# Where the transposed value products of an attention and FFN kernel are copied and normalised

## The reference

```python
q, k, v = split_heads(xn @ Wq + bq), split_heads(xn @ Wk + bk), split_heads(xn @ Wv + bv)   # 16 heads of 8
scores = einsum('bhqd,bhkd->bhqk', q, k) * 8 ** -0.5 + slopes[h] * rel[k]    # alibi, see below
ctx = einsum('bhqk,bhkd->bhqd', softmax(scores), v)
attention = ctx @ Wo + bo
# ffn: fp4_linear quantises both sides in blocks of 16 and multiplies
ffn = fp4_linear(silu(fp4_linear(xn, w_gate)) * fp4_linear(xn, w_up), w_down)
```

## Time and profile before

| What | us |
|---|---|
| median of 3 runs (lowest, highest) | 858.97 (858.61, 860.21) |
| profiled execution, its time | 858.46 |
| its span | 856.7 |
| PE busy | 778.5 (91%) |
| DVE busy | 695.4 (81%) |
| ACT busy | 652.2 (76%) |
| POOL busy | 416.5 (49%) |
| chain that ended last | PE 66%, DVE 17%, ACT 6%, POOL 6% |

### The profile page before, as it was taken

How to read it: one execution, slowest core, us unless ns; L and a number is a source line. 1 busy time by engine, 2 the same in 40 slices (tenths; PEclk the granted TensorE clock), 3 DMA queues, 4 the chain that set the end, 5 groups by cost and what they waited for, 6 DMA issues and landing times.

```text
span 856.7 us, 13894 instructions
## 1 busy us (share of the span) xinstructions
PE 778.5 (91%) x4939; PEld 232.0 (27%) x4939; DVE 695.4 (81%) x792; ACT 652.2 (76%) x1342; POOL 416.5 (49%) x413
## 2 busy tenths in 40 slices
PE   3289998989999999899899999999999999998986
PEld 2012232223232333222232333222222323232322
DVE  7797886888989897788888887888888898989710
ACT  4206886878888888778788888887888888888885
POOL 7365263482628373662545462761717362442442
PEclk9657998999999999989999999999999999999999
DMA  5920002013102010050101011050102000000000
GB/s 149 243 51 1 2 2 76 2 50 100 39 1 51 2 67 10 14 149 1 39 2 38 3 45 45 2 160 2 38 2 50 3 14 2 2 1 2 2 2 25
DMA packets 32828, 31.85 MB, mean 37 GB/s; under 512 B 4344, under 2 KB 26552, under 8 KB 32760
## 3 DMA queue, kind: packets, MB, share of 16 engines
q1 hardware_dynamic: 32760, 30.96, 13.4%
HBM read 15.91 MB, written 15.04 MB: 36 GB/s over the span
## 4 chain that ended last, share of the span: by engine, by line
PE 66%; DVE 17%; ACT 6%; POOL 6%; issue 3%; DMA 1%; SPq 0%; POOLq 0%; ACTq 0%; DVEq 0%
PE low L1078 23%; PE mx L1048 21%; DVE neg_max L934 13%; PE low L1067 6%; ACT probs L728 4%; PE low L1116 3%; PE low L1101 2%; PE low L1095 2%; PE low L1034 2%; PE mx L1127 2%; PE low L1108 2%; ACT pv_s L825 1%; POOL mb L537 1%; DVE am L905 1%; PE low L1030 1%
## 5 line engine op out<-in xcount | busy, mean ns | idle before, releaser
L934 DVE TENSOR_REDUCE neg_max<-mx 128x1 f32<-128x1024 f32 x512 | 614.1, 1220 | 99.5 <-PE mx L1048 91.4
L728 ACT ACTIVATE probs<-low 128x512 f32<-128x512 f32 x1024 | 558.7, 607 | 141.1 <-PE low L1067 135.2
L1048 PE MATMUL mx<-k_op,q_op 51*128 51x512 bf16 x1024 | 320.1, 398 | 42.0 <-DVE neg_max L934 21.8
L1067 PE MATMUL low<-q_op,k_op 53*128 53x512 bf16 x1024 | 334.4, 389 | 12.7 <-ACT probs L728 9.1
L1078 PE MATMUL low<-probs,v_op 128*32 128x512 f32 x2048 | 275.7, 611 | 0.3
L1048 PEld LDWEIGHTS mx<-k_op,q_op 51*128 51x128 bf16 x1024 | 61.8, 95 | 318.2 <-issue 171.5
L1067 PEld LDWEIGHTS low<-q_op,k_op 53*128 53x128 bf16 x1024 | 74.7, 93 | 91.6 <-ACT probs L728 81.9
L630 POOL CAST neg_parts<-neg_max 128x16 bf16<-128x16 f32 x31 | 6.8, 219 | 167.1 <-DVE neg_max L934 102.1
L537 POOL TENSOR_SCALAR mb<-mb 128x960 f32<-128x960 f32 (+2 forms) x17 | 58.7, 3456 | 27.5 <-DVE mb L925 26.2
L1078 PEld LDWEIGHTS low<-probs,v_op 128*32 128x32 f32 x2048 | 40.5, 108 | 67.5 <-issue 32.2
L618 POOL TENSOR_TENSOR x_s<-x_s,down_s 128x128 f32<-128x128 f32 x32 | 14.6, 455 | 80.5 <-ACT down_s L761 57.9
(11 more groups left out here) (128 smaller groups left out, 589.8 us busy)
## 6 DMA issues: line engine op xcount, KB each, us to landing
q_op<-q_rows SPq DMA_DIRECT2D x32, 192.0 KB, 3.8
k_op<-k_rows SPq DMA_DIRECT2D x32, 192.0 KB, 4.8
q_rows<-qp SPq DMA_DIRECT2D x8, 384.0 KB, 2.6
k_rows<-kp SPq DMA_DIRECT2D x8, 384.0 KB, 2.9
x_s<-in_L_attn_inputs_dram SPq DMA_DIRECT2D x8, 256.0 KB, 3.8
q_rows<-qp SPq DMA_DIRECT2D x8, 256.0 KB, 2.9
k_rows<-kp SPq DMA_DIRECT2D x8, 256.0 KB, 3.1
out_dram<-o_s SPq DMA_DIRECT2D x8, 256.0 KB, 2.6
```

The lines of the kernel that those rows point to most:

```text
L728: nc.scalar.activation(probs[U % 3][:, 2 * g + x, :], bank("exp", U, j), ACT.Exp).then_inc(st_free, 1)
L934: nc.vector.tensor_reduce(to, slot("max", pos)[:], AX.X, ALU.max, negate=True).then_inc(mx_free, 1)
L1048: ins = nc.tensor.matmul(slot("max", pos)[:, 512 * kh:512 * kh + 512], q, k, start=True, stop=True)
L1067: nc.tensor.matmul(bank("exp", U, j), k_op[quad][r, g, kt * P:(kt + 1) * P], q_op[quad][r, g, half * HALF:(half + 1) * HALF], start=True, ...
```

## The change

`pvT` leaves AT_END and IN_DVE_RING: it becomes a middle job whose transposes go to one of the three banks of the ring that ScalarE frees. ScalarE copies the bank back to `pv_s`, in SBUF (a new copy, 32 times, and the old content of `pv_s` has been read by then). VectorE's two operations become `context(m)`, run in the unit after the job's, behind the first maximum of that unit; they read `pv_s` and no longer PSUM, and signal a new semaphore `ctx_ok`. `ctxT` is asked for two units after the last pvT instead of one. The next copy of `pv` into `pv_s` waits for `ctx_ok`. Since the middle places are shared, the planner moves other jobs too.

```diff
--- before.py
+++ after.py
@@ -73,8 +73,8 @@
 CHUNKS = 2 * B * QUADS * UNITS
 HALVES = 2 * B * QUADS
 FFN_FIRST, FFN_LAST = 5, 237
-AT_END = ("turn", "pvT")
-IN_DVE_RING = ("pvT", "bvo")
+AT_END = ("turn",)
+IN_DVE_RING = ("bvo",)
 
 
 def turn_unit(m):
@@ -146,7 +146,7 @@
             assert U < parts_unit(g)
             put(max(U, QUADS * UNITS * (b - 1) + 2) + 1, "v", g)
     for hb in range(2 * B):
-        U = put(at["pvT", hb // 2 * 8 + 6 + hb % 2] + 1, "ctxT", hb)
+        U = put(at["pvT", hb // 2 * 8 + 6 + hb % 2] + 2, "ctxT", hb)
         for i in range(2):
             U = put(max(U, at["down", 2 * hb + 1, 1]) + 1, "wo", hb, i)
     return at
@@ -318,6 +318,7 @@
         hid_ok = sem("hid_ok")
         down_ok = sem("down_ok")
         out_ok = sem("out_ok")
+        ctx_ok = sem("ctx_ok")
         z_ok = sem("z_ok")
         pow_ok = sem("pow_ok")
         quant_ok = sem("quant_ok")
@@ -780,6 +781,9 @@
                     keep_v(p)
                 elif kind == "turn":
                     keep_turn(p)
+                elif kind == "pvT":
+                    full("pvT", p)
+                    nc.scalar.copy(pv_s[:], bank("pvT", p)).then_inc(st_free, 1)
                 elif kind == "ctxT":
                     full("ctxT", p)
                     if p:
@@ -821,7 +825,7 @@
                         m = U // KT - 1
                         act.wait_ge(pv_done, U - 1)
                         if m:
-                            act.wait_ge(mx_full, MX["pvT", m - 1] + 1)
+                            act.wait_ge(ctx_ok, m)
                         nc.scalar.copy(pv_s[:], pv).then_inc(pv_kept, 1)
                     for job in middle(U) if j == 1 else ():
                         job_on_scalar(job)
@@ -938,21 +942,22 @@
                     nc.vector.tensor_tensor(neg_parts[m % 2][:, 16:32], neg_max[m % 2][:], neg_parts[m % 2][:, 0:16],
                                             ALU.subtract).then_inc(parts_max_ok, 1)
 
+            def context(m):
+                b, quad, half = m // 8, m // 2 % QUADS, m % 2
+                dve.wait_ge(st_free, ST["pvT", m] + 1)
+                heads = pv_s[:].rearrange("p (t h c) -> p t h c", h=4, c=32)
+                if b >= 2 and quad == 0 and half == 0:
+                    dve.wait_ge(st_full, ST["ctxT", 2 * b - 3] + 1)
+                link(nc.vector.reciprocal(pv_r[:].rearrange("p (t h) -> p t h", h=4), heads[:, :, :, D]))
+                nc.vector.tensor_tensor(
+                    ctx_s[b % 2][:, 4 * half:4 * half + 4, 32 * quad:32 * quad + 32].rearrange(
+                        "p t (h d) -> p t h d", d=D), heads[:, :, :, 0:D],
+                    pv_r[:].rearrange("p (t h) -> p t h", h=4).unsqueeze(3).to_broadcast([P, 4, 4, D]),
+                    ALU.mult).then_inc(ctx_ok, 1)
+
             def job_on_vector(job):
                 kind, p = job[0], job[1] if len(job) > 1 else 0
-                if kind == "pvT":
-                    b, quad, half = p // 8, p // 2 % QUADS, p % 2
-                    full("pvT", p)
-                    heads = slot("pvT", p)[:, 0:512].rearrange("p (t h c) -> p t h c", h=4, c=32)
-                    if b >= 2 and quad == 0 and half == 0:
-                        dve.wait_ge(st_full, ST["ctxT", 2 * b - 3] + 1)
-                    link(nc.vector.reciprocal(pv_r[:].rearrange("p (t h) -> p t h", h=4), heads[:, :, :, D]))
-                    nc.vector.tensor_tensor(
-                        ctx_s[b % 2][:, 4 * half:4 * half + 4, 32 * quad:32 * quad + 32].rearrange(
-                            "p t (h d) -> p t h d", d=D), heads[:, :, :, 0:D],
-                        pv_r[:].rearrange("p (t h) -> p t h", h=4).unsqueeze(3).to_broadcast([P, 4, 4, D]),
-                        ALU.mult).then_inc(mx_free, 1)
-                elif kind == "bvo":
+                if kind == "bvo":
                     full("bvo")
                     link(nc.vector.tensor_tensor(bo_s[:], slot("bvo")[:, 0:P], bo_s[:], ALU.add))
                     dve.sem_inc(mx_free, 1)
@@ -986,6 +991,9 @@
                         job_on_vector(job)
                     if pos < CHUNKS:
                         reduce_chunk(pos)
+                    for job in JOBS.get(U - 1, ()) if i == 0 else ():
+                        if job[0] == "pvT":
+                            context(job[1])
                     for p in range(NP):
                         up0, up1 = AT["up", p, 0], AT["up", p, 1]
                         if (U, i) == (up0 + 1, 1):
@@ -1121,14 +1129,14 @@
                 elif kind == "turn":
                     turn(p)
                 elif kind == "pvT":
-                    free_slot("pvT", p)
+                    free_bank("pvT", p)
                     pe.wait_ge(pv_kept, p + 1)
                     for t in range(4):
-                        ins = nc.tensor.transpose(slot("pvT", p)[:, t * P:(t + 1) * P], pv_s[:, t * P:(t + 1) * P], ident[:])
-                    ins.then_inc(mx_full, 1)
+                        ins = nc.tensor.transpose(bank("pvT", p)[:, t * P:(t + 1) * P], pv_s[:, t * P:(t + 1) * P], ident[:])
+                    ins.then_inc(st_full, 1)
                 elif kind == "ctxT":
                     free_bank("ctxT", p)
-                    pe.wait_ge(mx_free, MX["pvT", p // 2 * 8 + 6 + p % 2] + 1)
+                    pe.wait_ge(ctx_ok, p // 2 * 8 + 6 + p % 2 + 1)
                     for t in range(4):
                         ins = nc.tensor.transpose(bank("ctxT", p)[:, t * P:(t + 1) * P],
                                                   ctx_s[p // 2 % 2][:, 4 * (p % 2) + t, :], ident[:])
```

## The result

| | before | changed |
|---|---|---|
| median of 5 runs each, us | 858.97 (856.29 to 860.21) | 862.96 (861.58 to 863.83) |
| ratio, 95% interval | | 1.0049 (1.0028 to 1.0069) |
| profiled execution, us / its span | 858.46 / 856.7 | 863.23 / 861.4 |

The account below looks back on a forecast made before the run. Neither DVE (81% busy) nor ScalarE (76%) fills the span, so the order of work matters. -3.5 - 6.0 - 4.8 + 12.9 + 4.6 + 0.6 = +3.8 us gave 862.8 us, range 855.5 to 868.

Parts of the forecast that it names:

- price list: Usual times between TensorE's value products, such as 2.46 us without a middle job and 2.95 with; 754.4 in all before.
- unit 40's pause: TensorE before hT of job 2: scale_back behind swish makes hT 3.6 us late, plus 2.0 for the clock: 5.6.
- unit 134's: TensorE before hT of job 8: scale_back behind swish makes hT 2.8 us late, plus 2.0 for the clock: 4.8.
- units 92 to 96: POOL's late hid there: up jobs move between its three_parts blocks, so 0.5 of 5.3 us stays, a gain of 4.8.
- pvT moves (-3.5): TensorE's units: 31 end jobs go (-18.0 us), 29 more middle jobs come (+14.2), plus 0.3; ScalarE's copies cost nothing extra.
- POOL's queue (+12.9): POOL's in-order work misses hT's new deadlines, with clock penalties behind the pauses: 5.6 + 4.8 + 1.7 + 0.8 us.
- The multiply waits for POOL (+4.6): DVE's multiply from SBUF waits out POOL's add in four contexts: 3.4 us, plus half of up to 2.4 for follow-up.
- DVE's share (-6.0): DVE's late small pieces shrink as pvT leaves the maxima's slots: 3.2 of 9.2 us stay.
- The clock: TensorE's clock drops behind a pause: 2.0 us added to each of two new stalls, 0.2 to the old one.
- rival 1: DVE's multiply does not wait for POOL: 858.2 us, range 856 to 860.5; chance 0.22 together with the nothing-moves rival.
- rival 2: POOL's late scale_backs do not bite in units 40 and 134, so the kernel is faster: 849 to 852 us; chance 0.15.
- rival 3: ScalarE becomes the bound, pvT units taking 3.3 us: 874, or 866 to 870 if the clock stays low; chance 0.13.

Follow-up runs that it names:

- e2: Changed kernel with the context (reciprocal and multiply) behind the second maximum of its unit instead of the first: 854.3 us, 0.9937 of before.
- e1: Changed kernel with POOL's scale_back put ahead of swish and the other follow-up work of the same unit: 848.88 us, 0.9875 of before.
- e3: Kernel before, pvT's old path kept, with the changed kernel's table of jobs (the plan alone): 860.39 us, 1.001 of before.
- e4: Kernel before with scale_back put ahead of swish: 858.6 us, 0.9998 of before.
- e8: Changed kernel with pvT in a middle place of its own, so nearly all other jobs stay as before (the path alone): 856.36 us, 0.9983 of before.
- e7: Changed kernel with ScalarE copying each pvT bank twice, once into a spare tile: 862.5 us, 1.0062 of before.
- e10: Repeat on one chip of the changed kernel with scale_back ahead of swish: 849.84 us, 0.9904 of before.
- e5: Changed kernel with scale_back ahead of swish and the context behind the second maximum: 845.65 us, 0.9874 of before.
- e6: Changed kernel with scale_back first, the context behind the second maximum, and three_parts of group 2 in units 22 and 24: 839.53 us, 0.9803 of before.
- e9: Kernel before with three_parts of group 2 in units 22 and 24 instead of 16 and 18: 854.28 us, 0.9958 of before.
- e11: Repeat on one chip of the changed kernel with scale_back first and the context behind the second maximum: 847.17 us, 0.9874 of before.
- e12: Repeat of the changed kernel, unedited, as base on one chip: 861.1 us, 1.0034 of before.

## Why the prediction was right

The number and the sign were right (862.8 against 862.96; the repeat lies 1.9 lower, at 861.1), and so were the places of nearly all of the cost. The closeness of the number is partly luck: the profiled pair owes 3.0 of its 4.8 to the start-up, and what the change itself did there is +1.8, not +3.8. Step by step, in us of excess over the price list, from the starts of the products in the changed kernel's profile:

| step | forecast | measured |
|---|---|---|
| unit 40's pause, clock included | 5.6 | 5.9 |
| unit 134's | 4.8 | 4.1 |
| job 1, units 19 to 21 | 4.5 + 1.7 = 6.2 | 6.2 |
| the multiply's direct waits | 4 x 0.85 = 3.4 | 3.4, in five units |
| its knock-on | 1.2 | in the rows above and below |
| units 92 to 96 | 0.5 | 0.4 |
| jobs 6 and 11 | 0.8 | 1.1 |
| small pieces elsewhere | 3.2 | 3.1 |
| the first interval | 1.3 as before | 0.9 |
| sum | 27.0 | 25.1 |
| the tail | +0.6 | +0.5 |

The small negative pieces are left out (with them the sum is the 24.7 of e2's section). The forecast is 1.9 above the measured sum, and this is why the profiled pair shows +1.8 and not +3.8.

- **pvT moves (-3.5)** held: each pvT unit takes 2.95, and DVE's idle time before the reciprocal fell from 34.9 to 22.6, all of that behind the last maxima. The list sums to 750.8 instead of 754.4. (The list prices the last interval at 2.95 before and 2.46 after, but it took 1.47 and 1.15. Unit 256 is past the last scores. That is why list and excess come out above the stretch of the products on both sides.)
- **POOL's queue (+12.9)** was right in place and cause and nearly in size, and e1, e3 and e4 show the cause: the plan alone makes the pauses, the order alone removes them, and on the old plan the order is worth nothing. The two sizes were right partly by luck. hT came 4.3 and 3.1 late (by its start against the product before it, less the usual 1.53) where 3.6 and 2.8 were forecast, and the clock took less than forecast (below). Unit 134's 4.8 was also reckoned without a stretched multiply; the plan alone gives about 2 there (e2, e3), and the other half came through DVE's blocked multiply, max_parts' wait and the clock.
- **The multiply waits for POOL (+4.6)**: the direct part is right to 0.1, though the four forecast units gave 2.9 and a fifth, 35, gave 0.6. The trace of before was read too narrowly here. It does hold a two-input DVE operation out of SBUF beside an add of POOL (58.91, last section), and the context's reciprocal, named for rival 1, read PSUM there. The knock-on of 1.2, "half of up to 2.4", was too small: in the jobs that it names (6, 8, 10 and 11) e2 gives back 3.5, of which 2.2 in unit 134. This and the smaller price of the clock, below, offset each other. Here the Trainium skill (SBUF — State Buffer, on the shared port pair) has the rule: a VectorE instruction with two SBUF inputs blocks behind a GpSimd one that reads SBUF, for all of it. The eight stretched multiplies of eight, against none of ten with the PSUM operand, agree with it. One row doesn't: in e8 a multiply ran its 0.29 beside POOL's tensor_scalar, which reads SBUF too. So what the runs show is narrower than the Trainium skill's rule: a wait for POOL's tensor_tensor.
- **DVE's share (-6.0)** held: 3.1 of the 9.2 stayed. The small operations gained next to nothing from reading SBUF, the multiply 0.29 as before and the reciprocal 0.24 instead of 0.26, against the 65 ns each of the prediction's estimate.
- **The clock.** It fell behind both new pauses, as forecast, but cost less than 2.0: unit 40 lost 5.9 for a lateness of 4.3, so 1.6, and unit 134 4.1 for 3.1, so 1.0. At unit 134 that was close: with 2.55 and 2.28 of idleness instead of 3.00 it did not fall at all (e3, e2), though at the turn of the earlier trace rows it fell after 2.40.
- **Rivals.** Rival 1 (no wait for POOL) falls by the eight multiplies; rival 2 (scale_back not late) by the pauses; rival 3 (ScalarE) by e7, with room to spare. Rival 2's time of 849 to 852 is what e1 and e10 measured (848.9 and 849.8), once the lateness was taken out by another order.

What the forecast did not have is the start-up difference. One pair of profiles can't size the change to better than about 2 us (e4), and the medians differ by 4.0 and 2.6; the runs bear out a slowdown of 0.19% to 0.69%. Whether it is nearer 1.8 or 3.8 stays open.

## What to carry to other kernels

When a planner moves jobs, write down for each in-order queue which item has a deadline and what now stands ahead of it: here swish could wait and scale_back could not, and one moved call was worth 1.3% of the time where the intended saving was 0.4%. Before an operand moves from PSUM to SBUF to free a bank, look which instructions of the other engine it will overlap: the multiply with two SBUF inputs waited out every GpSimd tensor_tensor that it met, and a late maximum can come back as a late queue on GpSimd. Mend the largest pause first and measure the second effect again: the same edit was worth about 8 us with the pauses and 2.7 without. And test the parts of a change apart: here the plan alone cost nothing clear, the path alone gained, and the loss came only with both.

## What the runs showed of the hardware that was not expected

**The start-up is decided in two places.** The first product lies at 73.2 to 73.5 in five of the fourteen profiles (before, e2, e4, e5, e6) and at 75.4 to 79.7 in the others, kernels with the old path (e3, e9) among them. The same kernel had 73.3 in e5 and 79.7 in e11. So it is not the change. The timelines of before and then of after, at the casts that load the bias rows (POOL, DVE, then the DMA that follows):

```profile
13.68 1.49 POOL L504 MEMSET q_op<- 128x1024 f32 x1
...
13.23 1.05 DVE L880 CAST probs<-probs 16x1024 bf16<-16x1024 f32 x1
...
15.55 0.33 SPq L447 DMA_DIRECT2D bias_rows<-probs  x1
```

```profile
13.68 0.94 POOL L505 MEMSET q_op<- 128x1024 f32 x1
...
13.23 3.73 DVE L884 CAST probs<-probs 16x1024 bf16<-16x1024 f32 x1
...
18.23 0.33 SPq L448 DMA_DIRECT2D bias_rows<-probs  x1
```

In the one, POOL's memset stretches to 1.49 and DVE's cast takes 1.05; in the other the memsets keep their 0.94, one behind the other, and the cast takes 3.73. The bias rows' DMA then starts 2.7 later, and the first product 3.0. One instruction of an engine can thus be kept waiting by several of the other, and which of them wins differs between executions. (DVE's two-input subtraction at 14.31 ran beside such a memset, which reads nothing, and took 1.21 as it does alone.)

The second place is the first turn, where DVE's subtraction for max_parts (two SBUF inputs) and an add of POOL start in the same hundredth of a us. First before, then e10:

```profile
58.91 3.66 POOL L543 TENSOR_TENSOR zb<-zb,mb 128x1632 f32<-128x1632 f32 x1
58.91 0.18 DVE L938 TENSOR_TENSOR neg_parts<-neg_max,neg_parts 128x16 bf16<-128x16 f32 x1
```

```profile
58.37 3.62 POOL L544 TENSOR_TENSOR zb<-zb,mb 128x1632 f32<-128x1632 f32 x1
58.37 3.64 DVE L943 TENSOR_TENSOR neg_parts<-neg_max,neg_parts 128x16 bf16<-128x16 f32 x1
```

A subtraction of 0.18 took 3.64, and the maxima behind it came 2.9 later. The two places account for all fourteen starts: neither late, 73.2 to 73.5 (five); only the cast late, 75.4 to 76.4 (after, e1, e3, e7, e8, e12); only the subtraction late, 76.2 (e10); both, 78.8 and 79.7 (e9, e11). No run was made to change either.

**A free copy.** ScalarE's recorded durations overlap: in e7 the first copy ends at 380.26, after the second starts (380.13), and that ends at 380.75, after the exponentials start (380.61). Summed durations overstate how full this engine is, and a whole second copy fitted into the unit of 2.95.
